# Moving layer-norm steps, first value products and the first row maxima in an attention and mixture-of-experts kernel

## The reference

```
x = x + layernorm(attention(layernorm(x)))       # x: 2 x 1024 x 512
x = x + layernorm(moe(layernorm(x)))

attention: q, k, v = h @ Wq + bq, h @ Wk + bk, h @ Wv + bv    (16 heads of 32)
   local : query block i (128 rows) sees keys 128 i - 64 .. 128 i + 192, softmax, times v
   global: rows 0, 1023 and the 62 queries with the largest norm see all keys;
           their result replaces the local one
moe: top-1 of 8 experts, 256 rows of room in each, silu(x W1) * (x W3) @ W2,
   times the gate, plus a shared expert of the same form
```

## Time and profile before

| what | value |
|---|---|
| median of three runs | 824.65 us |
| the profiled execution | 822.52 us, of which the span is 820.8 us |
| PE busy | 776.2 us, 95% of the span |
| DVE busy | 563.0 us, 69% |
| ACT busy | 422.9 us, 52% |
| POOL busy | 146.1 us, 18% |
| mean granted TensorE clock | 0.992 |

### The profile page before, as it was taken

One profiled execution on the slowest core, in us unless ns is written; L12 is line 12 of the kernel. 1 busy time (PEld: TensorE's weight loads), 2 busy tenths in 40 slices (PEclk: granted clock), 3 DMA queues, 4 the chain that ended last, 5 costly groups with the idle time before them and its releaser, 6 DMA issues.

```text
span 820.8 us, 13876 instructions
## 1 busy us (share of the span) xinstructions
PE 776.2 (95%) x5060; PEld 650.2 (79%) x5060; DVE 563.0 (69%) x1196; ACT 422.9 (52%) x839; POOL 146.1 (18%) x227
## 2 busy tenths in 40 slices
PE   6998999989999999998999999999999999999994
PEld 4786777777777777776878887999999999887883
DVE  5764798468888566777588545466776666758666
ACT  5464352445656565767544244566675666633120
POOL 3300010510111113332354432000000000013122
PEclk9999999999999999999999999999999999999998
DMA  7789565976775888872349622676778776546444
GB/s 233 230 275 346 167 187 168 276 199 174 190 202 156 204 215 234 230 198 92 105 149 312 233 98 94 186 230 200 219 237 237 227 237 221 171 146 204 138 155 141
DMA packets 117492, 162.39 MB, mean 198 GB/s; under 512 B 17364, under 2 KB 65236, under 8 KB 117424
## 3 DMA queue, kind: packets, MB, share of 16 engines
q1 hardware_dynamic: 113840, 153.54, 61.9%
q0 software_dynamic: 3584, 7.97, 3.3%
HBM read 107.24 MB, written 55.05 MB: 198 GB/s over the span
## 4 chain that ended last, share of the span: by engine, by line
PE 63%; DVE 19%; DMA 6%; ACT 5%; issue 4%; SPq 1%; POOL 1%; POOLq 0%; DVEq 0%; ACTq 0%
PE bank L163 40%; PE wide L163 17%; DVE MX L160 4%; PE wide L167 3%; PE bank L167 2%; DVE SG L160 2%; DMA XX<-scr_xd 2%; DMA scr_q<-hl 1%; DVE STC L281 1%; ACT PTG L145 1%; DVE GC L153 1%; DMA H2A<-scr_oe,FG 1%; DMA scr_qtok<-H2A 1%; DVE TV L744 1%; ACT PT L157 1%
## 5 line engine op out<-in xcount | busy, mean ns | idle before, releaser
L163 PE MATMUL wide<-W2H,HH 128*128 128x512 f32 x308 | 101.9, 396 | 0.5 <-ACT OUTR L145 0.5
L160 DVE TENSOR_REDUCE MX<-wide 128x1 f32<-128x192 f32 (+1 forms) x128 | 77.6, 646 | 19.4 <-PE wide L163 19.3
L157 ACT ACTIVATE PT<-bank 128x512 f32<-128x512 f32 x128 | 73.6, 593 | 28.5 <-PE bank L163 28.4
L157 ACT ACTIVATE SIL<-bank 128x256 f32<-128x256 f32 (+1 forms) x72 | 32.7, 454 | 97.8 <-PE bank L163 97.6
L149 DVE TENSOR_TENSOR SIL<-bank,SIL 128x256 f32<-128x256 f32 (+1 forms) x72 | 36.8, 511 | 63.8 <-ACT SIL L157 63.2
L163 PE MATMUL bank<-XT,W13H 128*128 128x256 f32 (+1 forms) x336 | 76.6, 322 | 0.0
L145 ACT ACTIVATE HH<-SIL 128x256 fp32r<-128x256 f32 (+1 forms) x72 | 35.2, 489 | 67.5 <-DVE SIL L149 67.5
L163 PEld LDWEIGHTS wide<-W2H,HH 128*128 128x128 f32 x308 | 58.5, 190 | 13.2 <-ACT OUTR L145 1.3
L149 DVE TENSOR_TENSOR HH<-SIL,HH 128x256 fp32r<-128x256 f32 (+1 forms) x72 | 37.0, 514 | 45.5 <-ACT HH L145 37.3
L163 PE MATMUL wide<-W2L,HH 128*128 128x512 f32 x168 | 66.6, 396 | 0.9 <-DVE W2L L149 0.7
L163 PEld LDWEIGHTS bank<-XT,W13H 128*128 128x128 f32 x336 | 55.0, 188 | 4.7
(11 more groups left out here) (253 smaller groups left out, 2007.5 us busy)
## 6 DMA issues: line engine op xcount, KB each, us to landing
R<-in_L_ffn_W_dram SPq DMA_DIRECT2D x48, 512.0 KB, 5.5
scr_q<-hl SPq DMA_DIRECT2D x16, 512.0 KB, 4.3
scr_k<-hl SPq DMA_DIRECT2D x16, 512.0 KB, 4.1
R<-in_L_ffn_sw_dram SPq DMA_DIRECT2D x12, 512.0 KB, 5.3
QSe<-scr_q SPq DMA_DIRECT2D x36, 128.0 KB, 3.6
KSe<-scr_k SPq DMA_DIRECT2D x36, 128.0 KB, 3.0
scr_v<-vt SPq DMA_DIRECT2D x16, 272.0 KB, 2.2
R<-_attn_hidden_states_dram SPq DMA_DIRECT2D x16, 256.0 KB, 3.8
```

The costliest lines, as they stand in the source:

```text
L157: return do("act", lambda g: g.activation(dst, src, fn, **kw), after)
L160: return do("dve", lambda g: g.tensor_reduce(dst, src, AXX, op), after)
L163: return do("pe", lambda g: g.matmul(ps, a, b, start=start, stop=stop, skip_group_check=True), after, mark=mark)
```

## The change

In `proj_group` the rule that picks the steps for `ln_work()` is one for all groups: c = 1 and 3. In group 0 it was c = 1 and 2 for the queries, and c = 0 and 1 for the keys. In the written order of group 0, `values_begin(j)` is now directly behind `ln_turn(j)` for each tile, and `values_end` and some other steps are moved. In `first_maxima`, head 0's maxima are transposed into `wide2` instead of a `pj` bank. Head 1's two halves come one step later, the second in `wide`, and its maxima are transposed at a new step 3, into `wide2`.

```diff
-                        if c in ((1, 2) if g4 == n == 0 else (0, 1) if g4 == 0 else (1, 3)):
+                        if c % 2 == 1:
                             ln_work()
...
                 if at == 0:
-                    row_shift(0, pj)
+                    row_shift(0, W_, 1)
...
                     load_head(2, kv_b0)
+                if at == 1:
+                    W_.busy[0] = qtp.busy[0] + m_nrm[-1:]
                     row_max(1, 0, 1)
-                if at == 1:
-                    row_max(1, 1, 1)
                 if at == 2:
-                    W_.busy[0] = qtp.busy[0] + m_nrm[-1:]
-                    row_shift(1, pj)
+                    row_max(1, 1, 0)
                     load_head(3, kv_b0)
+                if at == 3:
+                    row_shift(1, W_, 1)
...
             split_wv(0, "pool")
             ln_turn(0)
-            ln_turn(1)
             split_wv(1, "dve")
             split_wv(2, "pool")
             split_wv(3, "dve")
             values_begin(0)
+            ln_turn(1)
             ln_mean(2)
             ln_norm(2)
             ln_mean(3)
-            ln_norm(3)
             values_begin(1)
-            ln_turn(2)
             values_end(0)
             load_w(1, wk)
+            ln_turn(2)
+            ln_norm(3)
             ln_mean(4)
+            values_begin(2)
             values_end(1)
             ln_turn(3)
             split_w(0, 0)
             constants()
             k0 = zero_rows()
-            values_begin(2)
+            values_begin(3)
             values_end(2)
             split_w(0, 1)
             ln_norm(4)
             ln_mean(5)
-            values_begin(3)
             values_end(3)
```

## The result

The changed kernel takes 833.17 us in the median of five runs (830.14 to 836.89); the kernel before takes 824.64 us in its five (822.39 to 825.49). The ratio is 1.0127, with a 95% interval of 1.0102 to 1.0151: slower, by 8.4 to 12.5 us. (It is not the quotient of the two medians, 1.0103: on record are 25 runs of the changed kernel, with a median of 834.12 us.) The forecast was 830.9 us, with 826.5 to 836. The profiled execution took 837.23 us with a span of 835.5 us, 14.7 more than the span of before. That is more than the runs differ by, because this execution is at the slow end of its kernel's runs and that of before at the fast end.

A forecast was written before the change was run, and what follows sets the result against it. PE was taken to bound the kernel, busy for 776.2 of 820.8 us. The terms 4.75 + 0.8 - 0.8 + 1.6 = +6.3 us, on the median of 824.65, gave about 830.9 us, range 826.5 to 836.

The forecast's parts named there:

- rival (b): First products of group 0: the clock stays low through the start, 9 us more instead of 1.6; 838 us; chance 0.10.
- Part 1: Written order of group 0: three PE pauses of 1.7 us before values products; +4.75 us, bounds +3.5 to +6.5.
- Part 2: `ln_work` in group 0: 4.0 us pause before group 1's first product, partly taken back; +0.8 us (0 to +2.5).
- The stretch behind the fill: Group 1, behind the 4 MB zero fill: PE's four waits give back 2.7 us, no less than 1.0.
- The 0.5 for turn 5: Group 0, at 33.26: turn 5 one step later removes PE's wait of 0.53 for its norm; -0.5 us.
- Part 3: Handover to attention: the 1.11 us wait for a bank goes, head 1's later row is hidden; -0.8 us (-1.1 to 0).
- The clock: Behind the new PE pauses: one more fall of the granted clock, 3.5 us long; +1.6 us (0 to 4.8).
- (a): New PE pauses come, but no fall of the clock: +4.7 us, 829.3 us; chance 0.30.
- (c): Attention loop: DVE's earlier start takes waits off PE's path in each pass, up to 9.8 us; 821.2 us; chance 0.04.
- (d): PE's pauses are wholly covered by the stretch behind the zero fill; 825.5 us; chance 0.06.

The follow-up runs named there:

- e12_all: The whole change once more, against the kernel before: ratio 1.0113, 9.3 us slower.
- e1_order: The kernel before with the new written order of group 0 alone: ratio 1.0041, 3.4 us slower.
- e8_fill: The kernel before with the 4 MB zero fill issued behind the keys of group 2 instead of group 0: ratio 1.0039.
- e5_filler: The kernel before with the new `ln_work` rule and 15 unread matmuls filling TensorE's pause before group 1's first product: ratio 1.0001.
- e11_best: The kernel before with `ln_work` at c = 1 and 3 for group 0's queries only, and the score ring one bank on: ratio 0.9972, 2.3 us faster.
- e3_handover: The kernel before with the change of `first_maxima` alone: ratio 1.0035, 2.9 us slower.
- e4_rowfirst: The kernel before with the `first_maxima` change, and head 3's keys loaded behind head 1's row DMA: ratio 0.9996.
- e7_bank: The kernel before with only the attention part's score ring started one bank further on: ratio 1.0012.
- e2_lnwork: The kernel before with the new `ln_work` rule alone: ratio 0.9998.
- e9_fill_lnwork: The kernel before with the zero fill issued two groups later and the new `ln_work` rule: ratio 1.0085.

## Why the prediction was right or wrong

The time lies in the range and the sign was right, but one part had the wrong sign and the clock's price was too small; both errors made the forecast too low. The forecast was +6.3 us, and +8.5 (medians) or +10.5 (ratio) was measured. That it lies in the range is partly luck: the upper end of 836 was there for half of rival (b), which came only in small.

- **Part 1 (+4.75 us): right.** Pauses of 1.57 us where 1.7 were worked out, three of them, and the first projection 4.7 us late in e12_all, whose first tile landed as early as before's. By time 3.4 us (1.5 to 5.3). Not foreseen: the slow start lasted 1.4 us longer in one execution (e1_order). That nothing takes this loss back was right. The upper bound was added up wrongly: 4.75 and twice 0.69 are 6.1, not 6.5.
- **Part 2 (+0.8 us): right in mechanism, two terms off.** The pause was 3.63 us, not 4.0 (the terms of the forecast add up to a start at 54.50, not 54.45, which changes nothing). The stretch behind the fill gave back 3.2 us, not 2.7: the waits named in the earlier trace rows are 2.7, but each of the four holds PE up for more than its idle time. From 68.94 to 85.94 us PE takes 17.0 us over the stretch with the four waits, and 13.6 over the same instructions in e8_fill (69.06 to 82.69), 3.4 less. Without a fall the part costs nothing (e5_filler is 0.13 us ahead at the end of group 1's work). The 0.5 for turn 5 was right in the changed kernel, where turn 6 is moved too; e11_best shows that it hangs on that.
- **Part 3 (-0.8 us): wrong in sign. This is the step that failed.** The prediction put head 1's row "some 3 us later, and needed only four slots into the attention part. Hidden." Four slots are 3.5 us of PE from the first scores to the wait (177.59 to 181.05), and the row had 2.1 us on its way to SP and 5.1 to land. The trace of before showed all I needed: its slots, and loads on SP of 1.35 us for three. I counted the order on SP only for what became earlier, and never set the row's landing against its first reader. e3_handover costs 2.9 us; e4_rowfirst shortens the wait to 0.84 us by moving three loads. The wait of 1.11 us for `vt` did go, as forecast. The wait of 0.84 for head 0's maxima, which the prediction left standing, went too; it differs between executions (0.21 in e11_best).
- **The clock (+1.6 us): right in kind, short in size.** There were two falls of 6.8 us in the changed kernel, 6.1 us of lost work in all, behind the pauses of 3.63 and 3.67 us. The forecast had one fall of 3.5 us. The first of the two is that one, and cost 2.9 us because it lasted twice as long; the second stands behind the wait that part 3 missed. The pauses of 1.57 us brought none in any of the four profiles that have them. e5_filler and e4_rowfirst show the cause for each place: fill or shorten the pause, and the fall is gone. The prediction says that the rows show one fall in the whole span of before; its trace has a second, of 3.4 us, at 500.1 us. "TensorE: Matmul & The Clock Gate" (Part 1: The HAM clock gate) of the Trainium skill has the rule that idleness brings the slow clock back; the falls behind these two pauses agree with it.
- **The rivals.** (a) did not come: falls followed. (b) came only in small, as a start that stayed slow for one product more (e1_order). (c), that a lead at the door brings more in each pass, did not come. What the prediction set against it holds in part: in every profile but that of e8_fill the lead or lag over before stays within 0.05 us from head 4's shift to head 10's. Further on it changes at single waits: a lead of 1.0 us shrank to 0.3 in e7_bank, and one of 1.8 us in e11_best was 2.3 at the end. (d) held for part 2 alone.

The changed kernel's first profile, added up: 0.6 for the late tile; 5.0 for part 1, to the first projection; about -0.5 for part 2 without its fall, and 2.9 for the fall. That is 8.0 us behind at ACT's copy of the norms (94.30 against 86.26). The missing wait for `MX` gives 0.9 back, 7.1 at the first shift. Part 3 without its fall costs 1.8 and its fall 3.1: 12.0 us behind at head 4's shift (204.07 against 192.04). The other 2.7 us of the 14.7 came up later and were not tested: 1.4 in the attention loop, at single waits, and 1.2 behind the last shift, where this execution has three falls and that of before two.

## What to carry to other kernels

A product that stands directly behind the transpose of its own operand pays the copy and the subtraction in full on TensorE; put the work that needs neither between them, one whole turnaround ahead. When a small DMA is moved, set its landing, with every load in front of it on the queue, against its first reader, for the value that becomes late and not only for those that become early. And price a long pause of TensorE with a fall of the clock behind it: here 1.7 us when PE was back at work as the fall began, and 2.8 to 3.1 when it was not.

## What the runs showed of the hardware

- The granted clock fell behind each pause of 3.2 to 3.7 us (in the changed kernel twice, and once each in e2_lnwork, e3_handover, e9_fill_lnwork and e12_all), and behind those of 2.0 to 2.3 us in e8_fill, e9_fill_lnwork and e12_all. It fell behind none of the pauses of 1.57 us among the first products, and not behind the wait of 0.84 us in e4_rowfirst.
- The length of a pause alone does not decide. In the attention loop, among narrower products, a fall followed waits of 1.62 us (e12_all), 1.25 (e5_filler), 1.24 and 1.16 (e9_fill_lnwork) and 0.65 (e7_bank), and none followed one of 1.49 us in e8_fill, at 343.58.
- A fall that began while PE was idle lasted 6.83 us (three times), and one that began while it was at work 3.41 (all others, but for the one at the very end of each trace).
- A DMA of 4 KB was waited for until 5.1, 4.6 and 3.4 us after its issue behind six loads and a store (changed kernel, e3_handover, e12_all), and 2.5 us with three loads less (e4_rowfirst).
- Moving 4 MB of zeros from a stretch where it cost 3.3 us, with the DMA engines 99% busy, to a less busy one cost more than it saved: e8_fill is 3.3 us ahead at 83.00 and 4.5 behind at the first row shift, with two falls of the clock on the way.
